# One over the standard deviation of each layer norm: a power on GpSimd in place of ScalarE's square root and VectorE's reciprocal

## What is computed

```
def _layernorm(x, axis=-1, eps=1e-05):
    m = jnp.mean(x, axis=axis, keepdims=True)
    v = jnp.var(x, axis=axis, keepdims=True)
    return (x - m) / jnp.sqrt(v + eps)

x = x + _L0_attn_ref(_layernorm(x, axis=-1), ...)
x = x + _L0_xattn_ref(_layernorm(x, axis=-1), ctx_1024, ctx_1024, ...)
...
x = x + _L3_ffn_ref(_layernorm(x, axis=-1), ...)
```

## Time and profile before

| | |
|---|---|
| median of 3 runs | 1412.75 us (1411.47 to 1413.98) |
| the profiled execution: own time | 1413.62 us |
| its span | 1411.9 us |
| granted TensorE clock, mean | 0.875 of full |
| busy share of the span | PE 78%, weight loads 60%, VectorE 60%, ScalarE 43%, GpSimd 15% |
| instructions | PE 8419, VectorE 1956, ScalarE 1209, GpSimd 317 |

### The profile page before, as it was taken

The page is one execution under the profiler, slowest core; times in us unless marked ns, Lnnn a source line. Parts: engine busy times, 40 slices in busy tenths (PEclk is TensorE's granted clock), DMA queues, the critical chain, the costliest instruction groups (busy, mean ns, idle before and its releaser), DMA issues. The chain is left out here.

```text
span 1411.9 us, 21976 instructions
## 1 busy us (share of the span) xinstructions
PE 1106.4 (78%) x8419; PEld 852.0 (60%) x8419; DVE 850.8 (60%) x1956; ACT 612.1 (43%) x1209; POOL 216.8 (15%) x317
## 2 busy tenths in 40 slices
PE   6267775969987388699969988997569980776998
PEld 4234453559972256589947775776348860444997
DVE  4799965852334657562247785777676667765222
ACT  1188873754434146444414443444112223662443
POOL 1364523810000015220000000000210011201000
PEclk9589986979998578789979999999688985895999
DMA  8200000000000000000040000000200000000000
GB/s 313 51 1 1 1 1 0 2 2 1 1 1 1 0 2 2 1 1 1 1 190 1 1 1 1 2 1 9 112 1 1 1 1 0 1 1 1 0 1 16
DMA packets 10952, 25.65 MB, mean 18 GB/s; under 512 B 4104, under 2 KB 8832, under 8 KB 9568
## 3 DMA queue, kind: packets, MB, share of 16 engines
q1 hardware_dynamic: 10848, 24.24, 4.8%
HBM read 23.71 MB, written 0.52 MB: 17 GB/s over the span
## 5 line engine op out<-in xcount | busy, mean ns | idle before, releaser
L1184 ACT ACTIVATE arena<-bank,w_L_ffn_b1T 128x512 f32<-128x512 f32 x192 | 131.4, 688 | 148.3 <-PE bank L1128 147.4
L1210 DVE SCALAR_TENSOR_TENSOR x<-bank,gate_c,x 128x128 f32<-128x128 f32 x192 | 54.1, 345 | 209.6 <-PE bank L1169 209.6
L1128 PE MATMUL bank<-x_high,w_low 128*128 128x512 f32 x264 | 113.1, 428 | 11.5 <-DVE w_low L1137 11.5
L1169 PEld LDWEIGHTS bank<-bufA,arena 128*128 128x128 f32 x1024 | 118.8, 192 | 2.6
L1169 PE MATMUL bank<-bufA,arena 128*128 128x128 f32 x1024 | 119.4, 275 | 0.0
L1128 PE MATMUL bank<-x_high,w_high 128*128 128x512 f32 x264 | 107.1, 406 | 0.0
L1128 PE MATMUL bank<-x_low,w_high 128*128 128x512 f32 x264 | 106.2, 402 | 0.0
L459 ACT ACTIVATE arena<-arena 128x128 f32<-128x128 f32 x256 | 80.4, 394 | 42.7 <-DVE arena L467 42.7
L1806 ACT ACTIVATE arena<-arena 128x512 f32<-128x512 f32 x64 | 40.4, 631 | 123.7 <-DVE arena L1852 123.7
L272 PE MATMUL bank<-ident,xc 128*128 128x128 f32 x96 | 27.1, 464 | 55.7 <-DVE xc L251 55.7
L1128 PEld LDWEIGHTS bank<-x_high,w_low 128*128 128x128 f32 x264 | 52.1, 197 | 20.7 <-issue 11.8
(11 more groups left out here) (418 smaller groups left out, 2448.3 us busy)
## 6 DMA issues: line engine op xcount, KB each, us to landing
bufA<-in_L_ffn_w SPq DMA_DIRECT2D x4, 2048.0 KB, 10.2
bufB<-in_L_ffn_W SPq DMA_DIRECT2D x2, 2048.0 KB, 19.9
bufB<-in_L_ffn_Wgu SPq DMA_DIRECT2D x1, 2304.0 KB, 14.9
bufA<-in_L_attn_Wqkv SPq DMA_DIRECT2D x1, 2048.0 KB, 7.7
bufB<-in_L_ffn_Wd SPq DMA_DIRECT2D x1, 1152.0 KB, 17.1
arena<-in_L_attn_Wout SPq DMA_DIRECT2D x1, 1024.0 KB, 9.8
x<-in_x SPq DMA_DIRECT2D x1, 512.0 KB, 3.7
ctxT<-in_ctxT SPq DMA_DIRECT2D x1, 512.0 KB, 4.3
```

Source lines behind the costliest of these rows:

```text
L1128: m = pe.matmul(bank[:, :], a[:, ws], b[:, c], start=n == 0, stop=n == 2)
L1169: i = pe.matmul(bank[:, j * P:(j + 1) * P], h[:, f, j * P:(j + 1) * P], w2[:, u * FF + f * P:u * FF + (f + 1) * P], start=f == 0, stop=f = ...
L1184: act.activation(m["h"][k % 2][:, f, :], banks[f][:, :], ACT.Gelu, bias=b1[:, c:c + 1]).then_inc(g["hidden"].sem, 1)
L1210: dve.scalar_tensor_tensor(x_blk(4 * t + j), banks[4 + n % 4][:, j * P:(j + 1) * P], gc[:, 4 * t + j, u:u + 1], x_blk(4 * t + j), ALU.mult ...
```

## The change

The two steps on 128x8 numbers go to GpSimd, in front of each stage's own GpSimd function: it adds epsilon to the variances and raises the sum to the power of minus one half. VectorE loses two instructions per norm (L246, L248), and its semaphore `var` is now counted up by the eight `bn_aggr`; ScalarE loses the square root and the spare one ahead of it. A constant tile of -0.5 is filled at the start. One line more in the declarations moves all line numbers behind it by one (and those of the norm by a few).

```
+        mhalf = sb("minus_half", [P, NB])
...
-            ("var", 1), ("std", 1), ("xc", NB), ("turned", NB), ("xnA", 1), ("xnV", 1))} for st in STAGES}
+            ("var", NB), ("std", 1), ("xc", NB), ("turned", NB), ("xnA", 1), ("xnV", 1))} for st in STAGES}
...
-                         (blkneg, 0.0), (anyblk, 1.0)):
+                         (blkneg, 0.0), (anyblk, 1.0), (mhalf, -0.5)):
...
             for b in range(NB):
-                dve.bn_aggr(mean_var[:, b, :], parts[:, b, :]).then_inc(*dve_step.next())
-            dve.wait_ge(*dve_step.now())
-            dve.tensor_scalar(std[:, :], mean_var[:, :, 1], EPS, None, ALU.add).then_inc(n["var"].sem, 1)
+                dve.bn_aggr(mean_var[:, b, :], parts[:, b, :]).then_inc(n["var"].sem, 1)
             dve.wait_ge(*n["std"](1))
-            dve.reciprocal(rstd[:, :], std[:, :]).then_inc(*dve_step.next())
-            dve.wait_ge(*dve_step.now())
...
+        def norm_pool(pool, st):
+            n = norm[st]
+            pool.wait_ge(*n["var"](NB))
+            pool.tensor_scalar(std[:, :], mean_var[:, :, 1], EPS, None, ALU.add).then_inc(*pool_step.next())
+            pool.wait_ge(*pool_step.now())
+            pool.tensor_tensor(rstd[:, :], std[:, :], mhalf[:, :], ALU.pow).then_inc(n["std"].sem, 1)
...
-            act.activation(rstd[:, 0:1], blk01[:, 0:1], ACT.Sqrt)
-            act.wait_ge(*n["var"](1))
-            act.activation(std[:, :], std[:, :], ACT.Sqrt).then_inc(n["std"].sem, 1)
             act.wait_ge(*n["turned"](4))
...
             constants_pool(pool)
+            norm_pool(pool, "L0_attn")
             layer0_attention_pool(pool)
+            norm_pool(pool, "L0_xattn")
             layer0_cross_pool(pool)
...
+            norm_pool(pool, "L3_ffn")
             layer3_experts_pool(pool)
```

More of the change, by code:

```diff
@@ L2394, in _ @@
             constants_pool(pool)
+            norm_pool(pool, "L0_attn")
             layer0_attention_pool(pool)
+            norm_pool(pool, "L0_xattn")
             layer0_cross_pool(pool)
+            norm_pool(pool, "L0_ffn")
             layer0_experts_pool(pool)
+            norm_pool(pool, "L1_attn")
             layer1_recurrence_pool(pool)
+            norm_pool(pool, "L1_xattn")
             layer1_cross_pool(pool)
+            norm_pool(pool, "L1_ffn")
             layer1_experts_pool(pool)
+            norm_pool(pool, "L2_attn")
             layer2_attention_pool(pool)
+            norm_pool(pool, "L2_xattn")
             layer2_cross_pool(pool)
+            norm_pool(pool, "L2_ffn")
             layer2_experts_pool(pool)
+            norm_pool(pool, "L3_attn")
             layer3_attention_pool(pool)
+            norm_pool(pool, "L3_xattn")
             layer3_cross_pool(pool)
+            norm_pool(pool, "L3_ffn")
             layer3_experts_pool(pool)
```

## The result

| | before | after |
|---|---|---|
| median of 6 runs each | 1412.11 us (1411.38 to 1414.19) | 1435.68 us (1430.14 to 1438.22) |
| ratio, 95% interval | | 1.0155 [1.0138, 1.0172] |
| profiled execution, own time | 1413.62 us | 1430.14 us |
| its span, mean granted clock | 1411.9 us, 0.875 | 1428.1 us, 0.874 |

What follows compares the result with a forecast made beforehand. Each norm was taken as a line of single steps, every delay before the first `xc` paid twelve times. 5.9 + 8 - 0.2 + 0.2 = +13.9 us gave 1427.5, less 0.9 to the median 1426.7 us; range 1415 to 1443.

Steps and rivals of the forecast that it cites:

- Chain: From the aggregation's end to the first `xc`, each of twelve norms: 0.73 to 1.22 us, +5.9 us in all.
- the power: GpSimd's 128x8 power in each norm: 46 steps on 8 elements, 0.60 us, plus 0.22 for the instruction, 0.82 us.
- The upper bound of 1.96: Longest length allowed for the power in each norm, taken from GpSimd's 1024-element operation, 1.96 us.
- rival 1: The norms' power is long, 2 us and more; at 1.96 us +27.6 us, 1440 us; chance 0.15.
- Fills: GpSimd's fills, now behind the power, and `xc` shut each other out by turns: +8 us, between 3.9 and 13.2.
- The sign given for `L1_xattn`: In that norm, first `xc` over 1 us, the eight over 3.5 in place of 2.14, with fills between them.
- Collision in `L1_xattn`: The epsilon addition there met a running fill, 0.39 us in place of 0.17; this goes, -0.2 us.
- ScalarE: Around the norms, 14 table loads of 1.283 us less on this engine, costed at nothing because it waited anyway.
- rival 4: ScalarE's table loads were not hidden; all 14 exposed give -18, about -4 us in all, 1409 us; chance 0.05.
- First norm: The table load moves behind the wait for the transposes, delaying the first half of `xnT`: +0.2 us.
- Rival 2: The fills wait for `xc` and nothing is lost: +5.9 us, 1418.7 us, or 1411.5 with a cheap power; chance 0.13.
- rival 3: The norms' power costs an addition's 0.22 us: -1.3 us before `xc`, +6.7 with fills; with few fills in the way 0.09.

Runs made afterwards that it cites:

- e5_sizes: Kernel before, with dependent products and powers of 128x1 to 128x128 added on GpSimd in `L0_ffn`; its one run took 1409.7 us.
- e2_late: Changed kernel with GpSimd's larger fills in five stages held back until `xc` is complete; +16.7 us against before, ratio 1.0118.
- e6_both: Changed kernel with a multiplication by 0.02 for the power and the larger fills held back until `xc` is complete; +3.0 us against before, 1.0018.
- e3_noloads: Kernel before with both square roots replaced by copies, so the table loads around the norms go; +1.2 us, ratio 1.0008.
- e1_mult: Changed kernel with a multiplication by 0.02 in place of the power, fills left as they are; +10.1 us against before, ratio 1.0076.
- e8_halves: Changed kernel with larger fills held back and the power in two halves, `xc` starting after the first; +9.6 us against before, 1.0068.
- b1_bias: Kernel before with epsilon as the bias of ScalarE's square root in place of VectorE's addition; -0.7 us, ratio 0.9992.

## Why the prediction was right, and where it was off

Forecast 1426.7 us, measured 1435.7, inside the range (1415 to 1443) and slower, as given 83 in 100. The mechanism was the right one with both its parts; one term had the wrong size.

- **Chain, forecast +5.9 us, measured 16.8** (12 x 1.40; the collisions are counted below). The term that failed is the power, put at 0.82 us, measured 1.67; twelve times the difference is 10.2 us, more than the whole error of the sum (13.9 forecast, 23.6 measured). The addition was 0.24 for 0.20, the hand-overs 0.21 for 0.20. The power's work was sized as 46 steps of 1.62 ns per element; e5_sizes shows some 99. The fixed part, 0.22, was near the 0.31 measured. The upper bound of 1.96, from the nearest long row, held, and the truth lay much nearer to it than to my value: rival 1 (+27.6) was 4.0 us off, the forecast 9.7. A count of steps that no row supports should have moved the value up between its bounds, or the chance to rival 1.
- **Fills, +8, measured 6.9**, and by e2_late and e6_both nothing but them. The closeness of the sum is partly luck, for the detail was wrong in two ways that cancelled. I had the engines take turns, an instruction at a time; in `L1_xattn` and in two of the four stages with 128x512 fills they all passed first, in the others three of four. And the price of a block of fills is its length less about 0.55 us (2.69 to 2.15, 1.92 to 1.37), since the delayed `xc` ends 0.08 us behind the fills in place of its own 0.35, and those behind it close up (seven in 1.60 us in place of 1.79); small fills, to which I gave 0.1 us and more each, cost nothing. The sign given for `L1_xattn`, the first `xc` over 1 us and the eight over 3.5, held (2.69 and 4.29); "with fills between them" did not. The fills' later end cost nothing, as said.
- **Collision in `L1_xattn`, -0.2, measured -0.2:** its epsilon step now takes 0.24 us like the others. A second one, of 0.06 us, went from `L3_attn`, where the epsilon addition had taken 0.23 us in place of 0.17; the prediction counts the 390 ns as the one exception.
- **ScalarE, 0.** e3_noloads confirms it, with at most 0.4 us of gain by its interval; rival 4 falls.
- **First norm, +0.2, measured +0.36** (in the table it lies in the rest, since a norm is counted to VectorE's copy). The load does move behind the wait, as said; the timeline of the first norm:

```profile
13.08 1.28 ACT L265 ACT_TABLE_LOAD   x1 [13.08 <-PE bank L273]
13.93 0.69 DVE L251 COPY xnT<-bank 128x512 f32<-128x512 f32 x1 [0.57 <-PE bank L273]
14.38 0.60 ACT L265 ACTIVATE xnT<-bank 128x512 f32<-128x512 f32 x1
```

  ScalarE's half ends at 14.98, VectorE's at 14.62, and the first matmul of the stage waits for ScalarE's and starts at 15.03.
- **Rival 2** (fills yield) falls by `xc` at up to 4.29 us, **rival 3** (a power at an addition's price) by 1.67 us; e1_mult is what rival 3 would have been, and it is slower, as that rival said (+6.7 forecast, 6.1 in the norms, 10.1 timed, with the 4 us that stay open).
- **Not foreseen:** the rest of the span moves by some microseconds with the granted clock, in both directions, with the same matmuls; in both executions of the change `L3_xattn` and `L3_ffn` together were 3.4 and 2.6 us shorter than before.

The Trainium skill (SBUF — State Buffer, Who interferes with whom) says that GpSimd's use of the port pair it shares with VectorE locks it for a whole instruction, the loser blocking fully. For fills the trace agrees, even over several of them in a row (2.69 us), but the full 13.2 us that the prediction drew from this rule did not come: 6.9. For the power the trace does not agree with it: half a power runs 1.0 us beside `xc` in e8_halves with nothing lost. The skill's 6 us for a first call (GPSIMD Engine Reference, Instruction dispatch) did not show either: the first power started at 8.14 us, 0.08 us after the addition ahead of it, and took 1.67 us like all others.

## What to carry to other kernels

Before an operation moves to another engine, price it per element there, and if no row has it, measure it at the sizes used (the power took twice the guess here); work taken from an engine that nobody waits for (14 table loads here) pays nothing back. Look at what stands behind the moved instruction in the new engine's queue: the fills cost 0.3 us in all while they ran beside the statistics, 6.9 us once they started together with `xc`, and nothing when a wait put them behind it, since what reads them comes later. When the account by stretches and the timed difference are a few microseconds apart, compare the granted clock of the same stretch before inventing a mechanism.

## What the runs showed that was not expected

- A power on GpSimd costs 0.16 us per element of a partition, some 76 times a product's; a product of 128x8 takes 0.20 us.
- Going over GpSimd for a short step is no slower than ScalarE and VectorE together: 0.65 us from aggregation to `xc` with a product, 0.72 on the old road, 0.61 on the old road with one step less (b1_bias).
- A running power of 128x4 leaves VectorE's `xc` alone, while fills stop it, and the product of the earlier trace rows stopped a VectorE step of 1024 elements. That the power computes for most of its time and seldom touches SBUF would fit, but this is argued, not shown.
- Whether four fills in a row all pass ahead of `xc` or let it in between differs from execution to execution of one kernel; what decides it wasn't found.
